# A four-layer graph network: a second edge sort with its scatter and gather replaced by one-hot products over a list of tile and span pairs

## Chip, cores, metric

The kernel runs on one core of one Trainium2 chip. The metric is the device time of one execution in microseconds (us); lower is better.

## What is computed

A graph has 12,500 nodes with 128 features each and 212,500 directed edges (`src`, `dst`), in the order of `dst`. Four layers follow each other; after each the result is added to x and layer-normalised over the features.

```python
def _L1_gnn_ref(...):                      # the layer whose sums are changed
    def _gin_layer(x, src, dst, W1, b1, g1, be1, W2, b2, g2, be2):
        agg = jax.ops.segment_sum(x[src], dst, num_segments=x.shape[0])
        h = (x + agg) @ W1 + b1            # 128 -> 32
        h = _bn(jnp.maximum(h, 0.0), g1, be1)
        h = _bn(h @ W2 + b2, g2, be2)      # 32 -> 128
        return jnp.where(h > 0, h, NEG_SLOPE * h)
    h = _gin_layer(x, src, dst, W1_0, ...)
    return _gin_layer(h, src, dst, W1_1, ...)
```

Layer 0 sums `edge_val * x[dst]` by `src` and puts two branches behind it. Layer 2 runs a small MLP on every edge (`x[src]`, `x[dst]`, `edge_attr`) and sums by `src`. Layer 3 is an attention over the edges of each `src`. So layers 0, 2 and 3 sum by `src` and look up `dst`; layer 1, which has two GIN layers inside, sums by `dst` and looks up `src`. Since W1 is linear, layer 1 is computed on z = x @ W1, which has 32 features; z is held as three bf16 parts that add up to it (96 columns, `z3`).

## The kernel before

**Tiles.** The nodes are 98 blocks of 128. The edges are sorted by the block of `src` into `edges_a`, in DRAM, as 1,760 tiles of 128 edges, each tile with edges of one block (its number is in `blk_a`); an edge's row holds 128 attributes, `src` within its block, `dst` and the weight (`pay_a` in SBUF). Groups of 4 tiles are the step of all passes: 440 steps.

**First sort** (up to L1505). DVE makes a one-hot of the block (1,661 columns, one instruction for each of the 98 blocks, L1454), PE counts it (L1055), a scan gives the starts. Then the places are computed in five parts of the columns (`PARTS`), for each part 98 times: DVE compares (L1512), PE makes three products (L1075 to L1077), DVE takes the result where the one-hot is set (L1502). POOL may start to scatter once the first part (160 columns) is placed. It issues one indirect DMA for 128 edges (L775), 1,661 of them, in groups of ten; SP reads the attributes for each group (L654 on) and ACT puts the rest of the row beside them (`stage`, L848).

**Layer 0** (`sum_step`). POOL gathers x rows by `dst` (L807), one indirect DMA per tile; PE multiplies with a one-hot of `src` (L1127), DVE adds the result to the block's sums (L1625). Between its steps DVE and PE do the **second sort** for layer 1, by the block of `dst` (`hist_b`, `place_b`, `take_b`).

**First GIN layer.** POOL splits z into its three parts (`split`, L787). In each of 440 steps SP broadcasts the tiles' `src` (L690), DVE turns it into a one-hot (L1868), PE looks up z of the block by a product (L1240, with a block number that it loads into registers), ACT writes the message (L912, L913), and POOL scatters it to its place in `rows_b`, one indirect DMA per tile (L822). Then SP reads `rows_b` back in 110 chunks (L708), DVE makes one-hots (L1887), and PE adds to the sums in PSUM (`chunk_sums`, L1261), three products of 32 columns per tile.

**Second GIN layer.** z goes to DRAM (`z_tab`), POOL gathers it in the second order, one indirect DMA per tile (L834), and PE adds it up (`gather_sum`, L1276). Between the two and after them stand the dense parts (`gin_pe`, `gin_act`, `gin_dve`: two batch norms and the products with W2 and the next W1).

**Layers 2 and 3** (`mlp`, `attend`) run over `edges_a` again with a gather per tile each (L807, q_tab and h_tab). Between the layers stand node phases of 14 steps.

The order of the work is that of the program on each engine; semaphores set by hand tie the engines together. POOL issues its 10,460 indirect DMAs one after the other.

## Time and profile before

| | us |
|---|---|
| median of 3 runs | 16622.23 |
| lowest and highest run | 16610.61, 16624.17 |
| span of the profiled execution, first to last instruction | 14549.9 |
| POOL busy in it | 10118.0 (70%) |
| DVE busy | 6490.2 (45%) |
| PE busy | 5642.2 (39%) |
| ACT busy | 2071.4 (14%) |

The profile has one execution. It gives its span; a device time of its own, beside the span, is not given, so the only figure for what lies around the span is the median less the span, 2072 us.
### The profile page before, as it was taken

To read this page: it belongs to the slowest core of one execution; us is meant where nothing else is said; L and a number is where in the kernel's file an instruction comes from. 1 tells how busy PE (TensorE), PEld (TensorE's weight loads), DVE (VectorE), ACT (ScalarE), POOL (GpSimd) and SP (SyncE) were. 2 spreads that over 40 slices of the span, in tenths; PEclk is the share of its full clock that TensorE was granted. 3 is DMA by queue.
4 is the path that set the end of the run, shared out by engine and by line. 5 is a ranking of instruction groups with operands and counts; after the bars stand their busy time and mean duration, and the time that the engine had idled before them with its cause. 6 is when DMAs were issued, how large, how long until landed. Compare 5 with 4: busy or idle time off the path is not lost.

```text
span 14549.9 us, 185642 instructions
## 1 busy us (share of the span) xinstructions
PE 5642.2 (39%) x42509; PEld 4641.8 (32%) x42510; DVE 6490.2 (45%) x25163; ACT 2071.4 (14%) x8809; POOL 10118.0 (70%) x10603
## 2 busy tenths in 40 slices
PE   7200002546655111111441111127888885444443
PEld 2000002333334100000441111127888884444442
DVE  9201113667765100000541111137888886656666
ACT  0000000000002111111010000015666662000000
POOL 4777777777774677777237777746777774777775
PEclk9655555768765555555555555559999996555555
DMA  4444449211112212211321111125555554333333
GB/s 109 127 126 140 127 141 81 53 50 52 52 51 61 54 46 46 46 46 44 92 52 20 20 20 20 20 51 132 131 131 131 131 130 113 80 80 79 80 80 86
DMA packets 1400883, 1138.59 MB, mean 78 GB/s; under 512 B 445673, under 2 KB 1261295, under 8 KB 1400143
## 3 DMA queue, kind: packets, MB, share of 16 engines
q1 hardware_dynamic: 1049493, 567.59, 16.8%
q0 software_dynamic: 335264, 554.74, 15.6%
q10 hardware_dynamic: 15778, 12.82, 0.3%
q14 instruction: 276, 2.26, 0.1%
q8 instruction: 72, 1.18, 0.0%
HBM read 871.76 MB, written 262.57 MB: 78 GB/s over the span
## 4 chain that ended last, share of the span: by engine, by line
POOL 58%; issue 19%; DVE 4%; PE 2%; DMA 1%; ACT 1%; DVEq 0%; SPq 0%; POOLq 0%; ACTq 0%
POOL work L807 34%; POOL rows_b L822 12%; POOL work L834 11%; DVE work L1887 2%; DMA x_tab<-work 0%; DVE work L1849 0%; DVE work L1855 0%; PE ps L1261 0%; DVE work L1801 0%; PE ps L1357 0%; PE ps L1224 0%; PE ps L1229 0%; DVE work L1941 0%; PE ps L1218 0%; DVE big L1632 0%
## 5 line engine op out<-in xcount | busy, mean ns | idle before, releaser
L807 POOL DMA_INDIRECT work<-q_tab,pay_a x1760 | 1673.5, 951 | 715.8 <-issue 535.1
L807 POOL DMA_INDIRECT work<-h_tab,pay_a x1760 | 1671.8, 950 | 673.5 <-issue 536.1
L807 POOL DMA_INDIRECT work<-in_x_dram,pay_a x1760 | 1709.4, 971 | 545.2 <-issue 536.0
L822 POOL DMA_INDIRECT rows_b<-work,big x1760 | 1706.7, 970 | 540.0 <-issue 536.2
L834 POOL DMA_INDIRECT work<-z_tab,work x1760 | 1662.8, 945 | 539.2 <-issue 536.0
L775 POOL DMA_INDIRECT edges_a<-work x1660 | 1607.4, 968 | 567.0 <-issue 508.7
L1625 DVE TENSOR_TENSOR big<-big,ps 128x128 f32 (+1 forms) x5280 | 1494.7, 283 | 940.8 <-PE ps L1127 531.9
L1868 DVE TENSOR_SCALAR work<-work,iota_p 128x512 bf16<-128x512 bf16 (+1 forms) x1320 | 560.3, 425 | 2220.0 <-PE ps L1240 1946.5
L1431 PE MATMUL ps<-work 128*128 128x129 f32 x3520 | 916.9, 441 | 1220.5 <-DVE work L1617 1220.5
L1127 PE MATMUL ps<-work 128*128 128x128 f32 x3520 | 749.3, 379 | 1376.2 <-DMA work<-in_x_dram,pay_a 995.5
L1431 PEld LDWEIGHTS ps<-work 128*128 128x128 f32 x3520 | 788.2, 329 | 1256.5 <-DVE big L1625 1162.3
L1958 DVE TENSOR_SCALAR work<-iota_h,lo_chunk 128x128 bf16<-128x128 bf16 x1760 | 329.3, 270 | 1862.9 <-PE ps L1276 1858.1
L1617 DVE TENSOR_SCALAR work<-iota,work 128x128 f32<-128x128 f32 x3520 | 1134.8, 364 | 16.2
L1127 PEld LDWEIGHTS ps<-work 128*128 128x128 f32 x3520 | 639.3, 272 | 1561.9 <-issue 1495.5
L1276 PE MATMUL ps<-work 128*128 128x32 bf16 x5280 | 284.3, 194 | 1916.2 <-DMA work<-z_tab,work 1879.9
L1240 PE MATMUL ps<-big,work 128*128 x1760 | 292.0, 259 | 1878.7 <-ACT work L913 1864.6
L1276 PEld LDWEIGHTS ps<-work 128*128 128x128 bf16 x5280 | 238.2, 108 | 1962.4 <-issue 1957.7
L1393 PE MATMUL ps<-wc,work 128*128 128x128 f32 x3520 | 715.5, 285 | 355.8 <-ACT work L1010 187.1
L1240 PEld LDWEIGHTS ps<-big,work 128*128 128x128 bf16 x1760 | 183.3, 104 | 1987.4 <-issue 1946.7
L1394 PE MATMUL ps<-work,ident 128*128 128x128 f32 x3520 | 681.8, 275 | 0.0
L1395 PE MATMUL ps<-big,work 128*128 x3520 | 681.8, 275 | 0.0
L1393 PEld LDWEIGHTS ps<-wc,work 128*128 128x128 f32 x3520 | 533.1, 191 | 448.9 <-issue 223.6
(346 smaller groups left out, 12240.8 us busy)
## 6 DMA issues: line engine op xcount, KB each, us to landing
work<-lo_rows SPq DMA_DIRECT2D x1320, 128.0 KB
work<-edges_a SPq DMA_DIRECT2D x440, 256.0 KB
work<-in_edge_attr_dram SPq DMA_DIRECT2D x166, 640.0 KB, 5.1
rows_b<-work SPq DMA_DIRECT2D x80, 550.0 KB, 7.5
work<-rows_b SPq DMA_DIRECT2D x110, 400.0 KB, 3.2
work<-in_x_dram,pay_a POOLq DMA_INDIRECT x1760
rows_b<-work,big POOLq DMA_INDIRECT x1760
work<-z_tab,work POOLq DMA_INDIRECT x1760
```

Source lines behind the costliest of these rows:

```text
L775: pool.indirect_dma_start(out=edges_a, out_offset=bass.IndirectOffsetOnAxis(ap=stage_pos[:, k, j:j + 1], axis=0), in_=stage_a[:, k, j, :], ...
L807: pool.indirect_dma_start(out=ring[:, at:at + width], out_offset=None, in_=table, in_offset=bass.IndirectOffsetOnAxis(ap=pay[:, e, 1:2], a ...
L822: pool.indirect_dma_start(out=rows_b, out_offset=bass.IndirectOffsetOnAxis(ap=pos_b[:, s * G + j:s * G + j + 1], axis=0), in_=message[:, k ...
L834: pool.indirect_dma_start(out=rows_h[:, at:at + H3], out_offset=None, in_=z_tab, in_offset=bass.IndirectOffsetOnAxis(ap=pay_b_i[:, e, 1:2] ...
L1127: m = pe.matmul(ps[:, kk % 4, j * D:(j + 1) * D], lhsT=onehot[:, kk % 4, j], rhs=rows[:, at:at + D], start=True, stop=True)
L1393: pe.matmul(o, lhsT=attr_t[:, kk % 2, j * P:(j + 1) * P], rhs=wc[:, 2, :], start=True, stop=False)
L1394: pe.matmul(o, lhsT=ident[:, :], rhs=rows[:, at:at + D], start=False, stop=False)
L1395: m = pe.matmul(o, lhsT=onehot_t[:, kk % 2, j * P:(j + 1) * P], rhs=p_all[:, bass.ds(bl[j] * D, D)], start=False, stop=True)
L1431: m = pe.matmul(ps[:, sums + j // 2, (j % 2) * 256:(j % 2) * 256 + D + 1], lhsT=onehot[:, kk % 4, j], rhs=rows[:, at:at + D + 1], start=Tr ...
L1617: ins = dve.tensor_scalar(onehot[:, k % 4, j], iota[:, :], pst[:, k, j, 0:1], scale, ALU.is_equal, ALU.mult)
L1625: dve.tensor_tensor(o, o, tile_sums, ALU.add).then_inc(p.acc, 1)
L1868: dve.tensor_scalar(turned, lo_bc[:, k % 4], iota_p[:, 0:1], None, ALU.is_equal).then_inc(p.oht, 1)
```

## The change

**One sort.** The first sort now ranks by a cell, the block of `src` and the span of `dst` (25 spans of 512 nodes). Counting: DVE makes one-hots of 98 blocks and of 25 spans for 50 columns at a time (34 batches), PE multiplies them column by column (1,661 products of 98 x 25, L1183). Placing goes along with the scatter, a group of ten columns at a time (`ask`, `place`, `look`; L1598, L1616, L1196): SP broadcasts the keys of the group to all partitions (655 KB), DVE counts the edges of the same cell before each edge (ten instructions of 128 to 640 columns that also sum, L1623), PE fetches the start of each edge's cell (ten products) and DVE picks it (ten instructions of 50 columns that also sum, L1628). POOL waits for `ranks.placed` before each group's ten scatters. ACT issues the attribute loads now, and between the groups DVE, PE and ACT do the part of layer 0 that was done beside the scatter before (`own_step`, 14 of them, every eighth group from group 40).

**A list of pairs.** A tile's edges are in the order of their spans. Every pair of a tile and a span that has edges in it gets an entry; each span's entries are filled up to a multiple of 16. The bound on the list is 4,512 entries: 1,128 steps of 4, in 282 groups of 16. The list is made during layer 0 (`cell_list` to `pair_list`; 50 comparisons of 2,304 columns, L1841, with 18 small products each) in place of `hist_b` and `place_b`. After layer 0 POOL gathers the tile rows for it (36 indirect DMAs), and ACT and PE turn them.

**The two GIN sums.** For each step of 4 pairs (`pair_sums`) SP broadcasts the pairs' `src` (128 KB), DVE makes the turned one-hot (L2013) and four one-hots of 128 x 512 of `dst` in its span (L2016), PE looks up z (four products of 96 columns, L1381), ACT copies the messages (L1041), and PE multiplies them with the one-hots into 96 x 512 sums (four products of 512 columns, L1390). Every four steps DVE adds these to the sums (L2026). The sums of a node's own z come first (`own_columns`), and the dense part begins with `fold3`, 28 products of 448 columns in f32, in the place of 25 transposes. `rows_b`, `z_tab`, their scatters, gathers and reads are gone. All 4,512 entries are worked through in each layer.

```diff
+QG = 16
+QUADS_G = QG // 4
+PAIR_GROUPS = -(-((E + NB * (P - 1)) // P + NB * (SPANS - 1) + SPANS * (QG - 1)) // QG)
+PAIR_GROUPS += PAIR_GROUPS % 2
+PAIRS = PAIR_GROUPS * QG
+QUADS = PAIRS // 4
+QB = -(-PAIRS // P)
+QB += QB % 2
+HALF_B = QB // 2
...
+sp.wait_ge(ranks.stored, 32)
+for q in range(SGROUPS + 1):
+    wait(sp, ranks.placed, q - 3)
+    n = min(SG, COLS - q * SG)
+    sp.dma_start(row_bc[:, q % 4, 0:n, :].rearrange("p j f -> p (j f)"),
+                 key_rows[q * SG:q * SG + n, :].rearrange("j f -> (j f)").partition_broadcast(P)).then_inc(ranks.row_in[q % 4], 16)
...
+def pair_in(l):
+    def step(s, k, u):
+        wait(sp, sums.oht, s + (l * QUADS - 3))
+        sp.dma_start(pair_bc[:, k % 4, :], pair_lo[bass.ds(s * (4 * P), 4 * P)].partition_broadcast(P)).then_inc(sums.lo[k % 4], 16)
+    run_steps(sp, QUADS, RING, 0, step)
...
-for s in range(GROUPS):
-    k = s % RING
-    pool.wait_ge(z1.staged, 2 * s + 2)
-    for j in range(G):
-        pool.indirect_dma_start(out=rows_b, out_offset=bass.IndirectOffsetOnAxis(ap=pos_b[:, s * G + j:s * G + j + 1], axis=0),
-                                in_=message[:, k, j, :], in_offset=None).then_inc(got[k], 16)
...
-for c in range(TILES // CHUNK):
-    if c >= 5:
-        pool.wait_ge(p2.mm, 2 * GROUPS + (c - 4) * (CHUNK // G))
-    for j in range(CHUNK):
-        at, e = (c % 5 * CHUNK + j) * H3, c * CHUNK + j
-        pool.indirect_dma_start(out=rows_h[:, at:at + H3], out_offset=None, in_=z_tab,
-                                in_offset=bass.IndirectOffsetOnAxis(ap=pay_b_i[:, e, 1:2], axis=0)).then_inc(got[c % 5], 16)
+for s in range(SGROUPS):
+    k = s % 2
+    pool.wait_ge(order.attr[k], s // 2 * 16 + 16)
+    pool.wait_ge(order.staged, s * 3 + 3)
+    pool.wait_ge(ranks.placed, s + 1)
+    for j in range(SG):
+        pool.indirect_dma_start(out=edges_a, out_offset=bass.IndirectOffsetOnAxis(ap=pos_a[:, s % POS, j:j + 1], axis=0),
+                                in_=stage_a[:, k, j, :], in_offset=None).then_inc(order.scat[k], 16)
...
+pool.wait_ge(pairs.list, 1)
+pool.wait_ge(pairs.stored, 64)
+for b in range(QB):
+    pool.indirect_dma_start(out=got_rows(b), out_offset=None, in_=tile_rows,
+                            in_offset=bass.IndirectOffsetOnAxis(ap=tile_sel[:, b:b + 1], axis=0)).then_inc(pairs.got, 16)
...
+def message_out(l):
+    def step(s, k, u):
+        act.wait_ge(sums.smm, s + (l * QUADS + 1))
+        wait(act, sums.mm, s + (GROUPS + l * QUADS - 3))
+        act.activation(pair_msg[:, k % 4, :], ps[:, k % 4, 0:4 * H3], ACT.Copy).then_inc(sums.staged, 1)
+    run_steps(act, QUADS, RING, 0, step)
...
-def chunk_sums(s, k, u):
-    bl = load_blocks(ONLY_PE, blk_b, s, 2 * CHUNK)
-    for h in range(2):
-        c = 2 * s + h
-        pe.wait_ge(s1.oh, c * 4 + (GROUPS + 4))
-        pe.sem_inc(begun, 1)
-        for n in range(CHUNK // G):
-            for j in range(G):
-                for f in range(3):
-                    m = pe.matmul(ps_flat[:, bass.ds(bl[h * CHUNK + n * G + j] * H, H)], lhsT=onehot_h[:, 4 * h + n, j],
-                                  rhs=chunk[:, (2 * k + h) % 5, n * G + j, f * H:(f + 1) * H], start=False, stop=True, skip_group_check=True)
-            m.then_inc(s1.mm, 1)
...
+for c in range(width):
+    at = (m_ % 2 * PER + c // CG) * SPANS
+    m = pe.matmul(ps[0:NB, m_ // 2 % 8, at:at + SPANS], lhsT=hot[m_ % 3][:, 0:NB, c], rhs=hot[m_ % 3][:, NB:KEYS, c],
+                  start=c % CG == 0, stop=c % CG == CG - 1 or c == width - 1)
...
+def look(q):
+    pe.wait_ge(o.asked, q + 1)
+    wait(pe, o.placed, q - 3)
+    for j in range(min(SG, COLS - q * SG)):
+        m = pe.matmul(look_bank(q)[:, j * LOOK:(j + 1) * LOOK], lhsT=asked[0:NB, q % 2, j * P:(j + 1) * P],
+                      rhs=split_a[0:NB, q % 2 * 2 + j // CG, :], start=True, stop=True)
+    m.then_inc(o.look, 1)
...
+def pair_sums(l):
+    def step(s, k, u):
+        if live(s, QUADS):
+            bl = load_blocks(ONLY_PE, blk_row, s)
+            pe.wait_ge(sums.oht, s + (l * QUADS + 1))
+            wait(pe, sums.staged, s + (l * QUADS - 3))
+            for j in range(4):
+                m = pe.matmul(ps[:, k % 4, j * H3:(j + 1) * H3], lhsT=pair_turn[:, k % 4, j * P:(j + 1) * P], rhs=z3_flat[:, bass.ds(bl[j] * H3, H3)], start=True, stop=True)
+            m.then_inc(sums.smm, 1)
+        g, (kk, gu) = s - 2, back(k, u, 2, RING)
+        if live(g, QUADS):
+            pe.wait_ge(sums.staged, g + (l * QUADS + 1))
+            pe.wait_ge(sums.oh, g + (GROUPS + l * QUADS + 1))
+            if kk % QUADS_G == 0:
+                wait(pe, sums.acc, gu * 2 + (kk // QUADS_G + TILES + l * PAIR_GROUPS - 1))
+            for j in range(4):
+                m = pe.matmul(ps[0:H3, 4 + kk // QUADS_G, :], lhsT=pair_msg[:, kk % 4, j * H3:(j + 1) * H3], rhs=pair_hot[:, kk % 4, j, :],
+                              start=kk % QUADS_G == 0 and j == 0, stop=kk % QUADS_G == QUADS_G - 1 and j == 3)
+            m.then_inc(sums.mm, 1)
+    run_steps(pe, QUADS, RING, 2, step)
...
+for c in range(PCH):
+    for h in range(4):
+        at = h * PART + c * PW
+        m = pe.matmul(ps[:, c, 0:PW], lhsT=fold3[0:H3, h, :], rhs=acc_t[0:H3, at:at + PW], start=h == 0, stop=h == 3)
...
-if q < PLACED:
-    a, b = PARTS[q // NB]
-    s = q % NB
-    wait(dve, o.took, q - 7)
-    dve.tensor_scalar(eq_p[:, q % 8, 0:b - a], hi_h[:, a:b], iota[:, s:s + 1], None, ALU.is_equal).then_inc(o.eqp, 1)
-if q >= DEEP:
-    take_place(q - DEEP)
...
+for m in range(HBATCHES):
+    at, w = m * HB, min(HB, COLS - m * HB)
+    wait(dve, o.hist, m - 2)
+    dve.tensor_tensor(hot[m % 3][:, 0:NB, 0:w], hi_h[:, at:at + w].unsqueeze(1).to_broadcast([P, NB, w]), key_tab[:, 0:NB, 0:w], ALU.is_equal)
+    dve.tensor_tensor(hot[m % 3][:, NB:KEYS, 0:w], span_h[:, at:at + w].unsqueeze(1).to_broadcast([P, SPANS, w]), key_tab[:, NB:KEYS, 0:w],
+                      ALU.is_equal).then_inc(o.hot, 1)
...
+n = min(SG, COLS - q * SG)
+for g in range(-(-n // CG)):
+    k, first = q % 2 * 2 + g, first_a[0:NB, :, q * (SG // CG) + g]
+    ch.post(dve.tensor_scalar(quarter[0:NB, g, :], first, small[0:NB, 4:5], 0.25, ALU.add, ALU.mult))
+dve.tensor_scalar(asked[:, q % 2, 0:n * P].rearrange("p (j e) -> p j e", e=P), row_bc[:, q % 4, 0:n, P:2 * P], iota_p[:, 0:1], None, ALU.is_equal)
+ch.sync()
+for g in range(-(-n // CG)):
+    ch.post(dve.tensor_copy(split_a[0:NB, q % 2 * 2 + g, 0:SPANS], quarter[0:NB, g, :]))
+ch.sync()
+for g in range(-(-n // CG)):
+    at = split_a[0:NB, q % 2 * 2 + g, :]
+    ins = dve.tensor_tensor(at[:, SPANS:LOOK], quarter[0:NB, g, :], at[:, 0:SPANS], ALU.subtract)
+ins.then_inc(o.asked, 1)
+def place(q):
+    n = min(SG, COLS - q * SG)
+    dve.wait_ge(o.look, q + 1)
+    for j in range(n):
+        c, jj = q * SG + j, j % CG
+        w = (jj + 1) * P
+        dve.scalar_tensor_tensor(out=unread(q, j).rearrange("p (j e) -> p j e", e=P), in0=row_bc[:, q % 4, j - jj:j + 1, 0:P], scalar=cell_f[:, c:c + 1],
+                                 in1=earlier[:, (CG - 1 - jj) * P:CG * P].rearrange("p (j e) -> p j e", e=P),
+                                 op0=ALU.is_equal, op1=ALU.mult, accum_out=later[:, q % 2, j:j + 1])
+    for j in range(n):
+        c = q * SG + j
+        ins = dve.scalar_tensor_tensor(out=junk_x[:, P + j * LOOK:P + (j + 1) * LOOK], in0=iota_k[:, :], scalar=span_f[:, c:c + 1], in1=look_bank(q)[:, j * LOOK:(j + 1) * LOOK],
+                                       op0=ALU.is_equal, op1=ALU.mult, accum_out=found[:, q % 2, j:j + 1])
+    ch(ins)
+    if q >= POS:
+        dve.wait_ge(order.scat[q % 2], ((q - POS) // 2 + 1) * (16 * SG))
+    dve.scalar_tensor_tensor(out=pos_a[:, q % POS, 0:n], in0=found[:, q % 2, 0:n], scalar=4.0, in1=later[:, q % 2, 0:n], op0=ALU.mult, op1=ALU.add).then_inc(o.placed, 1)
...
+def compare(i):
+    h, k = divmod(i, SPANS)
+    wait(dve, pairs.mm, i - 3)
+    dve.tensor_scalar(cmp_q[i % 4][0:NB + 1, :], pair_h[0:NB + 1, :], pair0_h[0:NB + 1, h, k:k + 1], None, ALU.is_ge).then_inc(pairs.cmp, 1)
...
+def pair_sums(l):
+    def step(s, k, u):
+        if live(s, QUADS):
+            if k % 4 == 0:
+                dve.tensor_copy(pair_at[:, k * 4:k * 4 + 16], pair_dst[:, bass.ds(s * 4, 16)]).then_inc(sums.pst, 1)
+                dve.wait_ge(sums.pst, u * 2 + (GROUPS + l * (QUADS // 4) + k // 4 + 1))
+            dve.wait_ge(sums.lo[k % 4], u * 32 + (KEY_ROWS[k % 4] + l * per_sum + k // 4 * 16 + 16))
+            wait(dve, sums.smm, s + (l * QUADS - 3))
+            dve.tensor_scalar(pair_turn[:, k % 4, :], pair_bc[:, k % 4, :], iota_p[:, 0:1], None, ALU.is_equal).then_inc(sums.oht, 1)
+            wait(dve, sums.mm, s + (GROUPS + l * QUADS - 3))
+            for j in range(4):
+                ins = dve.tensor_scalar(pair_hot[:, k % 4, j, :], iota_s[:, :], pair_at[:, k * 4 + j:k * 4 + j + 1], None, ALU.is_equal)
+            ins.then_inc(sums.oh, 1)
+        g, (kk, gu) = s - 7, back(k, u, 7, RING)
+        if kk % QUADS_G == 0 and live(g, QUADS):
+            half = kk // QUADS_G
+            group = gu * 2 + half
+            v = load_span(group)
+            dve.wait_ge(sums.mm, g + (GROUPS + l * QUADS + QUADS_G))
+            wait(dve, sums.acc, group + (TILES + l * PAIR_GROUPS))
+            at = acc_t[0:H3, bass.ds(v * SPAN, SPAN)]
+            dve.tensor_tensor(at, at, ps[0:H3, 4 + half, :], ALU.add).then_inc(sums.acc, 1)
+    run_steps(dve, QUADS, RING, 7, step)
```

**Order on DVE.** In the pair loop of the changed kernel the last of each four steps, with the addition, is (work is the region with the one-hots, ps the PSUM, pair_dst the turned rows of `dst`):

```order
L2013 TENSOR_SCALAR work<-work,iota_p 128x512 [waits z_smm,lo_in3]
L2016 TENSOR_SCALAR work<-work 128x512 [waits sum_mm]
L2016 TENSOR_SCALAR work<-work 128x512 x3
L2000 TENSOR_LOAD work
L2026 ISA [waits sum_acc,sum_mm]
L2026 TENSOR_TENSOR big<-big,ps 96x512
```

The other three steps have the first three rows alone. Before, the chunk sums' part of DVE was, for two steps of four tiles:

```order
L1883 SCALAR_TENSOR_TENSOR work<-work 128x16 [waits z_payload]
L1887 TENSOR_SCALAR work<-iota_h,lo_chunk 128x128 [waits sum_mm]
L1887 TENSOR_SCALAR work<-iota_h,lo_chunk 128x128 x3
L1887 TENSOR_SCALAR work<-iota_h,lo_chunk 128x128 [waits sum_mm]
L1887 TENSOR_SCALAR work<-iota_h,lo_chunk 128x128 x3
```

A step has five instructions of 512 columns where it had four of 128, and no DMA of POOL stands beside it.

**Order on PE.** One step of the pair loop; ISA rows set the address of the next product from a register:

```order
L636 TENSOR_LOAD work
L1381 ISA [waits z_oht]
L1381 MATMUL ps<-big,work 128x96
L1381 ISA
L1381 MATMUL ps<-big,work 128x96
L1381 ISA
L1381 MATMUL ps<-big,work 128x96
L1381 ISA
L1381 MATMUL ps<-big,work 128x96
L1390 MATMUL ps<-work 96x512 [waits sum_oh,z_staged]
L1390 MATMUL ps<-work 96x512 x3
```

Before, the message pass had the first nine of these rows (L1240) for each step; the four products of 512 columns are new in the loop.

**Order on DVE while POOL scatters.** Before, the placing was a pair of rows for each of 98 blocks and five parts:

```order
L1512 TENSOR_SCALAR big<-big,iota 128x510 [waits sort_took]
L1502 COPY_PREDICATED big<-big,ps 128x510 [waits sort_took,sort_pos]
```

Now a group of ten columns has, in this order (a second five rows of L1623, like the first, are left out):

```order
L1605 TENSOR_SCALAR big<-work,small 98x25 [waits rank_asked,lo_in0]
L1605 TENSOR_SCALAR big<-work,small 98x25
L1606 TENSOR_SCALAR big<-pay_a,iota_p 128x1280
L1609 CAST big<-big 98x25 [waits s_sort]
L1609 CAST big<-big 98x25
L1613 TENSOR_TENSOR big<-big 98x25 [waits s_sort]
L1613 TENSOR_TENSOR big<-big 98x25
L1623 SCALAR_TENSOR_TENSOR big<-pay_a,big 128x128 [waits rank_look]
L1623 SCALAR_TENSOR_TENSOR big<-pay_a,big 128x256
L1623 SCALAR_TENSOR_TENSOR big<-pay_a,big 128x384
L1623 SCALAR_TENSOR_TENSOR big<-pay_a,big 128x512
L1623 SCALAR_TENSOR_TENSOR work,big<-pay_a,big 128x640
```

and, behind the second five, `L1628 SCALAR_TENSOR_TENSOR big<-big,ps 128x50 x10` and one row of L1633 that lets POOL go on. The placing has moved from ahead of the scatter to beside it.

## Rows read from the trace of the kernel before

**Rows 1.** The page's head, and the first line of its chain of waits.
```profile
span 14549.9 us, 185642 instructions
...
POOL 58%; issue 19%; DVE 4%; PE 2%; DMA 1%; ACT 1%; DVEq 0%; SPq 0%; POOLq 0%; ACTq 0%
```
**Rows 2.** Costliest groups on POOL: busy us, mean ns, idle before with its releasers.
```profile
L807 POOL DMA_INDIRECT work<-in_x_dram,pay_a x1760 | 1709.4, 971 | 545.2 <-issue 536.0 <-DMA pay_a<-edges_a 9.2
L822 POOL DMA_INDIRECT rows_b<-work,big x1760 | 1706.7, 970 | 540.0 <-issue 536.2 <-ACT work L912 3.8
L834 POOL DMA_INDIRECT work<-z_tab,work x1760 | 1662.8, 945 | 539.2 <-issue 536.0 <-DMA z_tab<-big 3.2
```
**Rows 3.** Stretches: length, busy us (count) of PE, PEld, DVE, ACT, POOL; clock, DMA share, GB/s.
```profile
0.00:184.30 184.30, 117.08 (x722) 58.90 (x723) 170.54 (x364) 2.20 (x9) 27.34 (x31) 0.90 0.50 99
184.30:2320.80 2136.50, 324.72 (x1486) 144.81 (x1485) 438.31 (x1202) 87.37 (x676) 1608.36 (x1662) 0.57 0.45 130
2320.80:4570.00 2249.20, 1188.06 (x5118) 810.76 (x5118) 1468.67 (x4512) 0.00 (x0) 1709.32 (x1760) 0.69 0.30 53
4570.00:4770.00 200.00, 124.67 (x624) 110.44 (x624) 140.61 (x568) 84.93 (x185) 27.41 (x56) 0.64 0.24 69
4770.00:7014.00 2244.00, 298.16 (x1766) 185.85 (x1766) 164.12 (x436) 263.31 (x878) 1706.73 (x1760) 0.50 0.19 46
7014.00:7405.00 391.00, 241.11 (x5268) 227.93 (x5269) 301.55 (x1870) 39.09 (x220) 0.00 (x0) 0.50 0.41 116
7405.00:7493.00 88.00, 68.09 (x299) 58.66 (x298) 50.02 (x100) 37.17 (x57) 30.74 (x56) 0.56 0.14 28
7493.00:9697.00 2204.00, 287.55 (x5289) 239.67 (x5287) 329.33 (x1836) 0.23 (x1) 1662.77 (x1760) 0.50 0.12 20
9697.00:9872.00 175.00, 99.55 (x537) 78.29 (x537) 126.37 (x394) 71.60 (x101) 0.30 (x1) 0.79 0.43 121
```
**Rows 4.** DVE groups by form: busy us, mean ns of one.
```profile
L1658 DVE TENSOR_SCALAR big<-big,iota 128x1760 bf16<-128x1760 bf16 x98 | 70.4, 718 | 0.1
L2006 DVE TENSOR_TENSOR work<-ps,gamma 128x512 f32<-128x512 f32 x440 | 290.1, 659 | 0.1
L1463 DVE TENSOR_TENSOR big<-big 128x1660 f32<-128x1660 f32 x1 | 1.9, 1890 | 0.0
```
**Rows 5.** Timeline of DVE, three stretches: start us, length us of the x instructions.
```profile
302.00 0.33 DVE L1512 TENSOR_SCALAR big<-big,iota 128x510 bf16<-128x510 bf16 x1
302.26 0.71 DVE L1502 COPY_PREDICATED big<-big,ps 128x510 f32<-128x510 uint16 x1
...
1225.07 1.89 DVE L1592 TENSOR_SCALAR big<-big 128x128 f32<-128x128 f32 x7
...
7018.41 2.69 DVE L1887 TENSOR_SCALAR work<-iota_h,lo_chunk 128x128 bf16<-128x128 bf16 x16
```
**Rows 6.** Timeline of one step of the message pass.
```profile
5608.37 0.49 ACT L912 ACTIVATE work<-ps 128x384 bf16<-128x384 f32 x1 [4.91 <-DMA rows_b<-work,big]
...
5609.27 0.66 PE L1240 MATMUL ps<-big,work 128*128 x4 [4.85 <-ACT work L913]
5609.97 0.35 DVE L1868 TENSOR_SCALAR work<-work,iota_p 128x512 bf16<-128x512 bf16 x1 [5.15 <-PE ps L1240]
...
5610.49 0.33 SPq L690 DMA_DIRECT2D work<-lo_rows  x1
```
**Rows 7.** PE: the placing stretch with its granted clock; 512-column groups by form.
```profile
184.00:460.00 276.00, 249.09 (x1143) 0.99 0.42 120
...
L1055 PE MATMUL ps<-big,onecol 128*128 128x512 bf16 x294 | 72.5, 390 | 26.4 <-DVE big L1454 26.4
L1249 PE MATMUL ps<-big,ident 128*128 128x512 f32 x24 | 15.7, 821 | 40.4 <-ACT work L913 39.9 <-ACT big L996 0.5
```
**Rows 8.** Timeline of ACT: an activation that also sums, and the next one.
```profile
10607.10 0.27 ACT L1019 ACTIVATE square<-ps 128x128 f32<-128x128 f32 x1
10607.26 0.20 ACT L1019 ACTIVATION_READ_ACCUMULATOR square<-ps 128x1 f32 x1
10607.35 0.28 ACT L1019 ACTIVATE square<-ps 128x128 f32<-128x128 f32 x1
```
**Rows 9.** Matmuls of 32 columns in the chunk sums.
```profile
7021.39 2.17 PE L1261 MATMUL ps<-work 128*128 128x32 bf16 x48 [39.59 <-DVE work L1887]
```

1290 lines of the change are left out of this document (643 added, 647 removed).

## The prediction

> **What bounds the kernel.** The page's head and its chain of waits come first: POOL is 58% of the chain and "issue" 19%, everything else is 7% or less [rows 1]. The costliest groups say what POOL does: indirect DMAs, each busy for 0.945 to 0.971 us, with 536 us of idle time per 1,760 of them put down to "issue", 0.30 us each [rows 2]. So POOL starts one every 1.25 to 1.27 us, and nothing on another engine ends those gaps. The windows by stage [rows 3] show where the span goes: 184.3 us ahead of the scatter, 2136.5 scatter, 2249.2 layer 0, 200 node phase, 2244 messages with their scatter, 391 chunk sums, 88 dense, 2204 gathers of z, 175 dense and node phase; then layers 2 and 3, which the change leaves as they are. In the scatter DVE is busy for 438 of 2136 us and PE for 325: both have room.
>
> The span is 14549.9 us, the median 16622.23. No device time of the profiled execution is given, so I make the sum as differences of its span and carry the 2072 us around it over unchanged.
>
> **Prices.** DVE, bf16, one source and scalars: 16 instructions of 128 columns in 2.69 us are 0.168 each; of 510 columns the next instruction starts 0.26 after it [rows 5]; 1,760 columns take 0.718 [rows 4]. So 512 columns cost 0.27. The slope is (0.26-0.168)/382 = 0.24 ns a column by the first two, (0.718-0.26)/1250 = 0.37 by the last two; I use 0.28. f32: 7 of 128 columns in 1.89 us, 0.27 each [rows 5]; 1,660 columns with two f32 sources take 1.89 [rows 4]; the adding of PSUM to SBUF, 512 columns, 0.66 [rows 4]. From 0.27 for 128 columns I split off about 0.14 fixed and 1.04 ns a column, which the 1,660 columns bear out, (1.89-0.14)/1660 = 1.05. PE: four products with register addresses take 0.66 us, 0.165 each [rows 6], in a stretch with its clock at 0.50 [rows 3]; 512 columns bf16 take 72.5/294 = 0.247 busy, in the stretch where the clock is high [rows 7]: at 2.4 GHz about 0.22 from one to the next, so at 1.2 GHz about 0.43. ACT writes a message in 0.49, SP issues a broadcast in 0.33 [rows 6].
>
> **Part 1: the two GIN sums.** The 4,512 pairs are all worked through, so a step's price decides. By engine, for four pairs:
> - DVE: 5 x 0.27 = 1.35; per four steps an address copy with its wait, estimated 0.25, and the addition 0.66, so 0.23 a step: 1.58.
> - PE's array: four look-ups of 96 columns, about 0.2 in all at full clock, and 4 x 0.22: 1.07. With the register loads and address settings (0.165 x 4, about 0.6 for the loads) the sequencer needs about 1.5.
> - ACT 0.6 (0.49 and a wait), SP 0.5; POOL nothing.
>
> DVE is the longest, and PE's sequencer stands just under it. Nothing is hidden under POOL any more, since POOL does nothing here. For two engines so near each other that hand four buffers back and forth I add 0.12: **1.70 us a step**, 1128 x 1.70 = 1918 us a layer. The bounds: 1.55, if the fixed part of an instruction is smaller than the four-buffer rows say; and 2.0, if queueing costs 0.4. Against it: first layer, -2244 - 391 + 1918 = **-717**. Second, -2204 + 1918 = **-286**. So two thirds of POOL's work in these stages is gone, and the gain is only a third of it.
>
> **Part 2: placing beside the scatter.** A group of ten columns must not take longer than POOL's ten scatters, 10 x 1.263 = 12.6 us [rows 2]. DVE's group: L1623 ten times, 3,840 f32 columns: 10 x 0.14 + 3840 x 1.04 ns = 5.4. L1628 ten times 50 columns: 1.9. Both also write their sums; the nearest rows are ACT's: an activation starts at 10607.10, its accumulator read at 10607.26 and the next activation at 10607.35 [rows 8]: of the read's 0.20 only 0.09 is added. Twenty of them, 1.8. `ask`: one of 1,280 bf16 columns 0.5 and six small at 0.17, 1.5. The last instruction and waits 0.4. Sum 11.0, under 12.6. One group in eight also carries an `own_step` of about 15 us of DVE's work: eight groups need 8 x 11.0 + 15 = 103 us against POOL's 101. They are level; what falls behind is caught up at 1.6 us a group before the next and after the last. I take **+20** for the stage, between 0 and +328 (rival 3). The broadcasts of 655 KB a group come on top of DMA engines that are busy for 0.45 of the stage [rows 3], and have three groups' time ahead.
>
> The Trainium skill, "VectorE: DVE Perf Modes", section "Two Vector instructions with no wait between them", states that an instruction that also writes out its accumulator runs as two, the main one and the read. It speaks against this change, and no DVE row here shows it. Without it the group would be 9.2 us by the sum above and the +20 would be 0; the +20 goes by ACT's pair of rows, as said.
>
> **Part 3: counting.** What stands ahead of the scatter today, 98 one-hots with 1,661 columns of counting and the first part's placing, is 184.3 us [rows 3]. Now 34 batches of 123 x 50 = 6,150 columns on DVE. Two bf16 sources: no such row, so from both sides: at the one-source slope of 0.28 ns a column 60 us, at the f32 two-source rate of 1.14 ns [rows 4] 236. PE's 1,661 products of 25 columns: 48 of 32 columns in 2.17 us are 45 ns each [rows 9], 75 us, up to 0.165 each [rows 6], 274. DVE and PE overlap; I take 150, near the middle, since two sources in bf16 lie between the two rows. With the keys, the scan of 2,450 columns x 34/10 (8,325 in all, 9) and the first group's look-up, 11, the first scatter starts at about 220: **+36**.
>
> The skill's same page, section "The perf-mode tier table", gives a two-source bf16 instruction twice the f32 rate, which would make the counting 34 x 3.5 = 119 us and the sum 31 lower.
>
> **Part 4: the list of pairs, in layer 0.** A step of four gathers is POOL's 5.05 us; DVE is busy for 1469 of 2249 us there and PE for 1188 [rows 3], and the work of the second sort leaves as that of the list comes. 50 comparisons of 2,304 columns, about 0.8 each, and 900 products of four columns fit: **0**. If DVE were full, +50. After layer 0 come 36 gathers (46 us of POOL, partly beside the 200 us of the node phase), their turning and the tables, +12 for what waits and +22 for `own_columns`, the copying of 98 blocks to 96 rows: **+34**. The bounds are 10 and 80.
>
> **Part 5: the dense parts.** `fold3`: 28 products of 448 f32 columns. Twelve f32 products of 512 columns show 15.7 us busy for 24 records, so 28 of 448 are 16 to 32 us [rows 7]; less the 25 transposes, +16. With the second layer's `own_columns` +13 and no z_tab to write (-5): first **+24**. The second, where a wait for z_tab doesn't exist: **+16**.
>
> **Sum.** 36 + 20 + 0 + 34 - 717 + 24 - 286 + 16 = -873. The span becomes 13,677, the time 16622 - 873 = 15,749.
>
> **The rivals.**
> 1. *Slower: PE's clock stays at 1.2 GHz in the pair loops.* For: in the chunk sums PE is busy for 241 of 391 us and its clock is 0.50 [rows 3]; in the pair loop it waits at each step for DVE or ACT. Then a step is 4 x 0.165 + 4 x 0.43 = 2.38 on PE, it becomes the bound at 2.4, and 2256 x 0.7 = 1579 us are lost: 17,330. It decides from 1.70 + 873/2256 = 2.09 us a step. Also layer 0 has 0.69. Against: the placing stretch, where products of up to 512 columns follow each other with waits for DVE between them as here, has 0.99 [rows 7]; the chunk sums' products have 32 columns.
> 2. *The queues cost more:* register loads, semaphores and the four buffers make it 2.0 a step. PE's own sum is near DVE's, and a late broadcast holds both. 2256 x 0.3 = 677: 16,430.
> 3. *DVE becomes the bound in the scatter.* If an accumulator read isn't overlapped (ACT's read alone 0.20, not 0.09 [rows 8]), a group is 11.0 + 20 x 0.11 = 13.2; 167 x 13.2 + 260 for the rest (14 own steps and the stage's ends) = 2464 against 2136 + 20: +308, 16,060. For: the sums of the two are only 1.6 us a group apart. Against: POOL's own distance of 1.25 us is steady, and an f32 row of 0.27 already holds its write.
> 4. *The time around the span falls with the indirect DMAs.* They go from 10,460 to 6,985, by a third; if the 2072 us were theirs, 690 go with them: 15,060. For: nothing in the trace says what it is. Against: nothing ties it to them either, and the distance of the DMAs inside the span stays as it is.
>
> The change can also fail to do what it says: if the pair loop still waited for POOL; but no POOL instruction stands in it, so I give that no chance of its own.
>
> **How the numbers follow.** Forecast 0.53 (15,750, its own range 15,400 to 16,050, with 1.55 and 1.83 a step), slower by the clock 0.08, queues 0.12, DVE in the scatter 0.15, time outside the span 0.10, and 0.02 left. A measurement of this kernel can tell about 0.2%, 33 us, from no change; of the cases only the first rival and the tail of the second are beyond that on the slow side: slower 0.09, same 0.01, faster 0.90. The range goes to the queues' 16,430 above; below, to 15,150, since 1.55 a step gives 15,410 and the fourth rival would need a bit more.
>
> **What would show it.** In the profile of the changed kernel: L2016 9,024 times, each 0.27 after the last; the two pair loops 1,918 us each, with DVE at over 85% there and PE's clock near 1.0 (0.5 is the first rival); L1390's products 0.22 apart. The first scatter at 220 us. In the scatter POOL waiting for `ranks.placed` by less than 1% of the stage; an average group above 12.6 us on DVE is the third rival. The gathers of layer 2 starting at 9872 - 873 = 9,000. And the median less the span again 2,072. The prediction is wrong if a step of the pair loop is over 2.09 us, or if a stage that I took as covered, the list of pairs or the broadcasts of keys, ends POOL's waits.

## The result and the profile after

| | before | changed | ratio (95% interval) |
|---|---|---|---|
| median, us | 16622.46 | 15473.67 | 0.931 (0.9299 to 0.9321) |
| span of the profiled execution | 14549.9 [rows 1] | 15486.0 | |
| its own time | not given | 15487.77 | |

The change is 1149 us faster; 873 were forecast. The two spans can't be compared: that of the changed kernel is its time less 1.8 us, that of before was 2072 us under its median. The kernel before, unchanged, takes 14,550 to 14,660 us in two groups of runs (here called the quick condition) and 16,610 to 16,650 in three (the slow one), so every ratio below is taken beside runs of the kernel before in the same group. The profile of the rows ahead of the prediction is of the quick condition, the times shown with it are of the slow one, and so is the result above. The ratio is 0.931 in both (0.9315, interval 0.9300 to 0.9331, in the quick one).

So the terms of the prediction, which came from the quick condition, are held against a profile of the changed kernel in that condition (its span is 13576.7, that of before 14557.0). Its stretches; the columns are those of [rows 3]: count and first place, scatter, layer 0, node phase and list, first pair loop, dense part with the second `own_columns`, second pair loop, dense and node phase:

```profile
0.00:384.10 384.10, 313.83 (x1733) 311.71 (x1734) 177.44 (x236) 49.41 (x31) 24.68 (x28) 0.54 0.25 60
384.10:2608.90 2224.80, 173.42 (x1960) 142.69 (x1960) 1584.88 (x8261) 72.36 (x511) 1697.87 (x1661) 0.51 0.51 152
2618.90:4849.30 2230.40, 929.93 (x4452) 814.66 (x4453) 1087.10 (x4064) 4.12 (x8) 1694.21 (x1759) 0.51 0.32 54
4849.30:5067.00 217.70, 146.29 (x761) 130.64 (x760) 150.99 (x602) 105.86 (x240) 64.51 (x93) 0.62 0.30 85
5067.00:6828.00 1761.00, 1648.52 (x9019) 894.35 (x9020) 1697.26 (x6202) 554.01 (x1128) 0.00 (x0) 1.00 0.32 84
6828.00:6938.00 110.00, 88.11 (x415) 69.91 (x413) 44.36 (x73) 42.85 (x68) 30.69 (x56) 0.67 0.02 5
6938.00:8701.00 1763.00, 1671.94 (x9030) 894.73 (x9028) 1698.46 (x6206) 554.72 (x1130) 0.00 (x0) 1.00 0.32 84
8701.00:8892.50 191.50, 116.78 (x572) 84.78 (x572) 124.57 (x391) 71.08 (x100) 0.00 (x0) 0.83 0.39 111
```

In a pair loop DVE is busy for 1697 of 1761 us and PE's clock is 1.00. Between the same marks (first and last indirect DMA of a stage, first one-hot of a pair loop) in the quick profiles of both kernels:

| stage | before | changed | difference | forecast |
|---|---|---|---|---|
| up to the first scatter | 183.1 | 384.1 | +201 | +36 |
| scatter | 2127.1 | 2224.8 | +98 | +20 |
| layer 0 | 2248.5 | 2230.4 | -18 | 0 |
| to the first GIN sum | 206.6 | 217.6 | +11 | +34 |
| first GIN sum, dense | 2722.7 | 1872.3 | -850 | -693 |
| second GIN sum, dense, node | 2384.3 | 1953.3 | -431 | -270 |
| layers 2 and 3, rest | 4674.6 | 4684.2 | +10 | 0 |
| sum | | | -980 | -873 |

Costliest groups that answer to [rows 2] and [rows 4], by form, of the changed kernel in the quick condition (busy us, mean ns, idle before):

```profile
L2016 DVE TENSOR_SCALAR work<-work 128x512 bf16<-128x512 f16 x9024 | 2557.6, 346 | 1.2 <-PE ps L1390 1.2
L859 POOL DMA_INDIRECT edges_a<-work,big x1660 | 1697.9, 1023 | 550.6 <-issue 505.3 <-DMA edges_a<-big,fill_pos 24.0 <-DMA work<-in_edge_attr_dram 17.6
L1183 PE MATMUL ps<-work 128*98 128x25 bf16 x1661 | 304.7, 342 | 1.8 <-ACT big L936 1.8
L1569 DVE TENSOR_TENSOR work<-work 128x4900 bf16<-128x4900 bf16 x33 | 89.5, 2713 | 172.1 <-PE ps L1183 172.1
L1570 DVE TENSOR_TENSOR work<-work 128x1250 bf16<-128x1250 bf16 x33 | 26.5, 803 | 0.0
```

**Counting.** PE is busy for 304.7 us and idle for 1.8; a product starts every 304.7/1661 = 0.183 us. The middle of the counting, same columns as above, with a clock of 0.50:

```profile
30.00:330.00 300.00, 300.00 (x1638) 300.00 (x1638) 105.27 (x64) 38.01 (x16) 0.00 (x0) 0.50 0.15 28
```
DVE, which makes the one-hots, waits 172.1 us for PE. What is long in a product is the load of its weights, in ns (least, median, most), of L1183 and, for comparison, of L1201, whose weights have 128 columns:

```profile
L1183 PEld LDWEIGHTS ps<-work x1661: 260/280/284, 28.0 to 332.3; 128*98 128x98 bf16 x185
L1201 PEld LDWEIGHTS ps<-big x1661: 95/119/151, 359.4 to 3309.0; 98*128 98x128 bf16 x185
```

After the last product (332 us) come the scan, the fill and the wait of 24.0 us for the fill to land, and the first scatter is at 384.1.

**The pair loop**, timeline of the quick profile: the rows of DVE follow each other without a gap but for the last one, where it waits 0.21 for its own copy of the positions, once in four steps.

```profile
5606.77 0.35 DVE L2013 TENSOR_SCALAR work<-work,iota_p 128x512 bf16<-128x512 bf16 x1
5606.93 0.49 ACT L1041 ACTIVATE work<-ps 128x384 bf16<-128x384 f32 x1 [0.97 <-PE ps L1381]
5607.03 1.14 DVE L2016 TENSOR_SCALAR work<-work 128x512 bf16<-128x512 f16 x4
...
5608.08 0.35 DVE L2013 TENSOR_SCALAR work<-work,iota_p 128x512 bf16<-128x512 bf16 x1
5608.20 0.60 PEld L1390 LDWEIGHTS ps<-work 128*96 128x96 bf16 x4
5608.21 1.06 PE L1390 MATMUL ps<-work 128*96 128x512 bf16 x4
...
5609.99 0.17 DVE L2009 CAST work<-pair_dst 128x16 f32 x1
5610.37 0.35 DVE L2013 TENSOR_SCALAR work<-work,iota_p 128x512 bf16<-128x512 bf16 x1 [0.21 <-DVE work L2009]
```

A step without the addition is 5608.08 - 5606.77 = 1.31 us, five instructions of 0.26; the mean is 1.562 (a loop of 1762 us by 1,128 steps).

**The first measurement** (slow condition) has one thing that the quick one doesn't. What POOL and ACT waited for in its scatter stage (us in total, times, longest):

```profile
POOL edges_a L859 <- DMA work<-in_edge_attr_dram: 677.6, 15, 51.7
POOL edges_a L859 <- issue: 497.5, 1619, 3.8
POOL edges_a L859 <- DVE big L1633: 89.5, 22, 10.7
...
ACT big L970 <- DVE big L1666: 942.7, 14, 70.2
```

and one of the 13 waits of 47 to 52 us, first ACT's timeline, then POOL's:

```profile
1207.30 0.20 ACT L952 ACTIVATE work<-big 128x10 f32<-128x10 f32 x1
1276.56 0.21 ACT L970 ACTIVATE big<-big 128x7 f32<-128x7 f32 x1 [69.05 <-DVE big L1666]
1276.56 0.37 ACTq L958 DMA_DIRECT2D work<-in_edge_attr_dram  x1
...
1230.34 0.95 POOL L859 DMA_INDIRECT edges_a<-work,big  x1 [0.30 <-issue]
1281.40 1.94 POOL L859 DMA_INDIRECT edges_a<-work,big  x1 [50.11 <-DMA work<-in_edge_attr_dram]
```

ACT now issues the attribute loads. Four groups ahead of each `own_step` it waits for DVE's variance (L969), and the next group's load stands behind that wait. When DVE isn't four groups ahead of POOL, the wait outlasts the groups that are loaded, and POOL stops at 1231 us until the load has landed. That this is the cause was tested by moving the wait (the runs with the later square root, below).

### The profile page after: what moved, and what is told of

It reads as the page before. It is cut to its first block and busy times, and to the rows that moved or that the text cites. A ratio compares the mean times of both kernels' runs of the same rounds, so it can differ in the third digit from the quotient of the medians.

```text
span 15486.0 us, 239207 instructions
## 1 busy us (share of the span) xinstructions
PE 8370.8 (54%) x49340; PEld 6322.0 (41%) x49341; DVE 9889.6 (64%) x39917; ACT 2938.7 (19%) x9899; POOL 6932.9 (45%) x7116
## 5 line engine op out<-in xcount | busy, mean ns | idle before, releaser
L2016 DVE TENSOR_SCALAR work<-work 128x512 bf16<-128x512 f16 x9024 | 2564.3, 349 | 1.5 <-PE ps L1390 1.5
L1390 PE MATMUL ps<-work 128*96 128x512 bf16 x9024 | 2392.2, 388 | 4.0 <-DVE work L2016 0.2
L859 POOL DMA_INDIRECT edges_a<-work,big x1660 | 1687.3, 1016 | 1291.4 <-DMA work<-in_edge_attr_dram 677.6
L1265 PE MATMUL ps<-work 128*128 128x128 f32 x3520 | 908.5, 435 | 1536.5 <-DVE work L1757 671.4
L1041 ACT ACTIVATE work<-ps 128x384 bf16<-128x384 f32 x2256 | 1105.5, 490 | 2414.4 <-PE ps L1381 2414.4
L1201 PE MATMUL ps<-big 98*128 98x50 f16 x1661 | 99.1, 218 | 2550.9 <-DVE big L1613 1520.4
L1972 DVE TENSOR_SCALAR work<-work,iota_p 128x512 f32<-128x512 bf16 (+1 forms) x880 | 383.5, 436 | 1703.8 <-remote 1629.3
L1265 PEld LDWEIGHTS ps<-work 128*128 128x128 f32 x3520 | 777.4, 322 | 1657.6 <-issue 1428.0
L1381 PE MATMUL ps<-big,work 128*128 x9024 | 1335.4, 212 | 199.5 <-DVE work L2013 182.5
L1381 PEld LDWEIGHTS ps<-big,work 128*128 128x128 bf16 x9024 | 862.5, 96 | 1175.2 <-issue 890.9
L1540 PEld LDWEIGHTS ps<-work 128*128 128x128 f32 x3520 | 788.1, 329 | 1115.2 <-DVE big L1765 651.3
L1390 PEld LDWEIGHTS ps<-work 128*96 128x96 bf16 x9024 | 927.7, 122 | 559.4 <-issue 14.2
L1201 PEld LDWEIGHTS ps<-big 98*128 98x128 bf16 x1661 | 78.5, 118 | 2573.0 <-DVE big L1613 1537.2
```

The costliest lines, as they stand in the source:

```text
L859: pool.indirect_dma_start(out=edges_a, out_offset=bass.IndirectOffsetOnAxis(ap=pos_a[:, s % POS, j:j + 1], axis=0), in_=stage_a[:, k, j, : ...
L1041: act.activation(pair_msg[:, k % 4, :], ps[:, k % 4, 0:4 * H3], ACT.Copy).then_inc(sums.staged, 1)
L1265: m = pe.matmul(ps[:, kk % 4, j * D:(j + 1) * D], lhsT=onehot[:, kk % 4, j], rhs=rows[:, at:at + D], start=True, stop=True)
L1381: m = pe.matmul(ps[:, k % 4, j * H3:(j + 1) * H3], lhsT=pair_turn[:, k % 4, j * P:(j + 1) * P], rhs=z3_flat[:, bass.ds(bl[j] * H3, H3)], s ...
L1390: m = pe.matmul(ps[0:H3, 4 + kk // QUADS_G, :], lhsT=pair_msg[:, kk % 4, j * H3:(j + 1) * H3], rhs=pair_hot[:, kk % 4, j, :], start=kk % Q ...
L1540: m = pe.matmul(ps[:, sums + j // 2, (j % 2) * 256:(j % 2) * 256 + D + 1], lhsT=onehot[:, kk % 4, j], rhs=rows[:, at:at + D + 1], start=Tr ...
```

## Experiments

**Two conditions.** The kernel before, unchanged, twice:

> The kernel before, unchanged, to see where the 2072 us lie that its median has above the span of the profile. Theory A (the time lies inside the stages: the profiled execution shown was free of stalls that the timed runs have): the span here is about 16,620, within 10 us of its own time, and the indirect DMAs of the unchanged layers 2 and 3 take longer than 2214 and 2206 us, like the 2680 and 2555 of the changed kernel. Theory B (the time lies around the span): a span near 14,550 again, with its time 2072 above it.

Measured: 14559.04 us, span 14557.0. Neither theory as written: the span is near 14,550, but so is the time. Nothing lies around the span.

> The kernel before, once more, for a profile under the conditions in which it takes 16,620 to 16,640 us. If it takes that here: Theory A says that its span is within 10 us of its time and that the 2072 us lie as stalls inside the stages in which POOL issues indirect DMAs, more per stage in layers 2 and 3 (about 450 and 350, as in the changed kernel) than in those with little on PE and DVE. Rival B: they lie in all stages alike, by the number of indirect DMAs (0.198 us each, 350 us a pass). If it takes 14,560 here, nothing new is expected.

Measured: 16642.05 us, span 16640.0. Theory A holds. Stretches of layer 2 and layer 3 in this profile, to be held against 2207.5 and 2206.4 us in the quick one:

```profile
11108.10:13792.90 2684.80, 2113.69 (x15562) 1952.37 (x15563) 1667.42 (x6889) 1334.18 (x6040) 1758.15 (x1759) 0.94 0.41 107
13953.50:16507.10 2553.60, 1034.01 (x5232) 917.58 (x5231) 1348.69 (x6088) 89.51 (x436) 1670.33 (x1760) 0.50 0.31 69
```

| stage length, us | before quick | before slow | changed quick | changed slow |
|---|---|---|---|---|
| scatter | 2127.1 | 2447.7 | 2224.8 | 2954.7 |
| layer 0 | 2248.5 | 2551.3 | 2230.4 | 2509.4 |
| messages / pair loop 1 | 2241.6 | 2505.4 | 1762.6 | 1761.4 |
| z gathers / pair loop 2 | 2198.1 | 2507.0 | 1761.7 | 1762.0 |
| layer 2 | 2207.5 | 2684.8 | 2210.8 | 2678.1 |
| layer 3 | 2206.4 | 2553.6 | 2212.0 | 2554.5 |

In the kernel before, the slow condition costs each of the six stages in which POOL issues indirect DMAs 264 to 477 us, 2021 of the 2083 us between the two profiles; the other 62 lie in the node phases between and behind them, and the stretch ahead of the scatter (183.1 and 183.0 us) and that from the last message to the first z gather (481.1 in both) have none of it. A pair loop has none either; the scatter of the changed kernel has 730. The change takes 264 + 309 = 573 us of it away and gives 730 - 321 = 409 back in the scatter; that is why the ratios are alike. What the condition is stays open. In its traces consecutive instructions of an engine often start 1.40 us apart, or 0.70 or 2.10: from 700 to 2300 us in the changed kernel DVE has 220 distances of 1.30 to 1.45 us and 49 of 2.0 to 2.2, and in the quick profile none of either; in the message stage of the kernel before, from 5500 us on, PE has 217 of 1.30 to 1.45 in 2000 us, and none in the quick profile. It wasn't tried whether this is a matter of the supply of instructions. The two quick groups ran on two chips and two of the slow ones on two others, so whether the condition belongs to the chip is open too.

**The changed kernel again**, quick:

> The changed kernel, unchanged, beside the kernel before on the same chip. Theory A (the 1104 us of stalls in the first measurement of the before/after pair, 2072 in the kernel before, belong to the conditions of that measurement and not to the kernels): if the kernel before takes 14,560 here, this one takes 13,565 (the run with two one-hots plus what its pair loops saved, 13,359 + 116 + 90), a ratio of 0.931 again; if the kernel before takes 16,620 here, 15,470. Rival B (the changed kernel always stalls once per own_step): 14,100 or more beside 14,560.

Measured: 13577.78 beside 14576.12, ratio 0.9315. Theory A; B is out, there is no wait for an attribute load over 10.4 us in it. And slow:

> The changed kernel, unchanged, as the mark for the run with the earlier address copy on the same chip: 13,565 to 13,580 us beside 14,560 of the kernel before, or 15,470 beside 16,620.

Measured: 15493.77 beside 16635.61, ratio 0.931 (0.9295 to 0.9326).

**ACT's wait four groups later.**

```diff
-                i, at = divmod(s + 4 - OWN_AT, OWN_GAP)
+                i, at = divmod(s - OWN_AT, OWN_GAP)
                 if at == 0 and 0 <= i < NSTEPS:
                     act.wait_ge(own.var, i + 1)
...
```

> Changed kernel, ACT's wait for DVE's own_step stands four groups later in ACT's order, behind the attribute load of the same group. Theory A (the 12 stalls of POOL of about 49 us, once in eight groups, come from attribute loads queued on ACT behind its wait for own_step): they go, the scatter stage falls from 2953 us to about 2350, the time to about 14,900. Rival B (DVE's own slow stretches hold the placing and the wait on ACT only shows them): the stage stays within 150 us of 2953, and POOL's waits move from the attribute load to ranks.placed. DVE, not ACT, would then be the bound.

Measured: 13575.12, but beside 14563.87: the quick condition, in which POOL isn't stalled, so it tells nothing of the theory. Its times were expected for the slow one.

> ACT's wait for own_step four groups later, now timed beside the unchanged changed kernel. Theory A: where POOL is not stalled by the attribute loads (12 to 15 waits of 49 us absent in the changed kernel's trace) this is within 0.2% of it; where they are there, 500 us or more faster. Rival B: slower by 14 x a few us everywhere, since DVE waits longer for the square root.

Measured: 13581.94 beside 13577.78 of the unchanged one: equal within 0.2%. The other half of Theory A needs the slow condition, below.

**Two one-hots of four**, and its counterpart, **two sum products of four**:

```diff
-                            m = pe.matmul(..., rhs=pair_hot[:, kk % 4, j, :], ...)
+                            m = pe.matmul(..., rhs=pair_hot[:, kk % 4, j // 2 * 2, :], ...)
...
-                        for j in range(4):
+                        for j in range(0, 4, 2):
                             ins = dve.tensor_scalar(pair_hot[:, k % 4, j, :], ...)
```

> Changed kernel; in the pair loops DVE makes two of the four one-hots of a step and PE uses each twice, so the sums of the two GIN layers are not those of the reference. Theory A (DVE bounds the loop at 1.56 us a step): a step falls to PE's price, between 1.07 (array) and 1.50 (its dispatch as predicted), so each loop by 70 to 550 us. Rival B (the hand-over of buffers or PE's dispatch bounds it): the loops stay within 2% of 1762 us.

Measured: 13359.48; a step is 1.459 us in the first loop and 1.481 in the second. Theory A, near its lower end. DVE's work was cut by 0.52 us and only 0.08 to 0.10 came: PE, busy for 98% of the stretch from 5500 to 6500 us, now bounds the loop at 1.46 to 1.48, near the 1.5 of the prediction, and DVE bounds the changed kernel's loop by the little in between.

```diff
-                        for j in range(4):
+                        for j in range(0, 4, 3):
                             m = pe.matmul(ps[0:H3, 4 + kk // QUADS_G, :], ...)
```

> Changed kernel; in the pair loops PE makes two of the four 512-column products of a step, so the sums of the two GIN layers leave out half of the pairs. Theory A (DVE bounds): the loops stay at 1762 us within 1%. Rival B (PE's array or its dispatch bounds): the loops fall by up to 2 x 0.22 x 1128 = 500 us each. What its clock does with fewer columns is seen too: if it falls to 0.5 and the loops still take 1762, the first rival of the prediction is too high for this kernel.

Measured: 15510.49 beside 16635.61; loops of 1761 and 1760 us. Theory A. A stretch of 1000 us inside the first loop:

```profile
6300.00:7300.00 1000.00, 838.07 (x3848) 381.21 (x3847) 964.65 (x3527) 314.77 (x641) 0.00 (x0) 0.78 0.32 84
```

The clock falls to 0.78 and the loop keeps its time; PE, with half of the long products, is busy for 838 of 1000 us and still keeps up. This isn't the first rival's case, which has all of the products.

**POOL makes the fourth one-hot.** DVE makes three; PE waits for both.

```diff
...
+                    wait(pool, sums.mm, s + (GROUPS + l * QUADS - 3))
+                    pool.tensor_scalar(pair_hot[:, k % 4, 3, :], iota_s[:, :], pair_at[:, k * 4 + 3:k * 4 + 4], None, ALU.is_equal).then_inc(own.relu, 1)
...
+                        pe.wait_ge(own.relu, g + (NSTEPS + l * QUADS + 1))
...
-                        for j in range(4):
+                        for j in range(3):
                             ins = dve.tensor_scalar(pair_hot[:, k % 4, j, :], ...)
```

> Changed kernel; POOL, idle in the pair loops, makes the fourth one-hot of each step. Theory A (DVE bounds a step at 1.56, PE at 1.46 as the run with two one-hots showed): a step takes 1.46 to 1.48, the two loops lose 190 us. Rival B (POOL's own instruction and its use of what it shares with DVE cost more): POOL needs over 1.5 us for 512 columns or DVE's instructions beside it lengthen, and the loops are slower than 1762 us.

Measured: 14694.17 beside 13577.78 of the changed kernel, 1116 slower; a step is 2.064. Rival B, in both of its halves. The group on POOL (busy us, mean ns, idle before):

```profile
L915 POOL TENSOR_SCALAR work<-work 128x512 bf16<-128x512 f16 x2256 | 3637.6, 1626 | 1035.0 <-DVE work L2021 903.1 <-PE ps L1402 115.5 <-issue 15.0
```

and in the timeline DVE's three one-hots beside it, which take 1.45 on average here and 0.87 in the changed kernel:

```profile
7002.92 1.65 DVE L2028 TENSOR_SCALAR work<-work 128x512 bf16<-128x512 f16 x3
```

What POOL would need with DVE at rest wasn't measured.

**DVE instructions beside POOL's DMAs.** In the changed kernel's scatter POOL's DMA takes 1.023 us on average, before 0.968 (L775). Sorted by what DVE does meanwhile, counted over the trace (profile of the kernel with the later square root, quick): the 783 that overlap an L1623, with two SBUF sources, take 1.095 on average; the other 877 take 0.961, those beside L1628 alone, whose second source is PSUM, 0.958. Tested in the kernel before:

```diff
                 turned_onehot(z1, k, u, onehot_th[:, k])
+                for q in range(4):
+                    ins = dve.scalar_tensor_tensor(out=spare[:, q, :], in0=onecol[:, :], scalar=1.0, in1=onecol[:, :], op0=ALU.is_equal, op1=ALU.mult)
...
                 ins.then_inc(p2.oh, 1)
+                for q in range(4):
+                    ins = dve.tensor_scalar(spare[:, q, :], onecol[:, :], 1.0, None, ALU.is_equal)
```

> Kernel before, with four added DVE instructions of 256 columns in each of 440 steps: two SBUF sources (the form of L1623) beside the message scatter, one SBUF source (bf16, the form of L2016) beside the gathers of z. Theory A (POOL's indirect DMA is lengthened while DVE runs an instruction with two SBUF sources, as 1.095 us beside L1623 and 0.957 without say): the message scatter's DMAs lengthen from 0.970 by about 0.05 on average, the stage by 40 to 120 us, the gathers of z stay at 0.945. Rival B (the key broadcasts on the DMA queues lengthen them): both stages unchanged.

Measured: 14651.56 beside 14576.12, in one run. Its groups, for [rows 2]'s L822 and L834:

```profile
L823 POOL DMA_INDIRECT rows_b<-work,big x1760 | 1774.5, 1008 | 540.2 <-issue 536.3 <-ACT work L914 3.8
...
L835 POOL DMA_INDIRECT work<-z_tab,work x1760 | 1682.1, 956 | 539.3 <-issue 536.2 <-DMA z_tab<-big 3.2
```

The message stage went from 2241.6 to 2309.8 us (+68), within Theory A's 40 to 120. The z stage wasn't unchanged: +19, 0.956 for 0.945, so one source lengthens POOL's DMA as well, by less per added us of DVE (19 us for 228 more of DVE's busy time, 68 for 580: 0.08 and 0.12). So the first half of Theory A holds, and its second half, with two sources alone, does not. Rival B is out as the only cause, since no key broadcast runs here; what share broadcasts have in the changed kernel's scatter wasn't tested.

**The address copy one step earlier.**

```diff
+                dve.tensor_copy(pair_at[:, 0:16], pair_dst[:, 0:16]).then_inc(sums.pst, 1)
...
                         if k % 4 == 0:
-                            dve.tensor_copy(pair_at[:, k * 4:k * 4 + 16], pair_dst[:, bass.ds(s * 4, 16)]).then_inc(sums.pst, 1)
...
+                        if k % 4 == 3:
+                            half = (k // 4 + 1) % 2
+                            dve.tensor_copy(pair_at[:, half * 16:half * 16 + 16], pair_dst[:, bass.ds((s + 1) * 4, 16)]).then_inc(sums.pst, 1)
```

> Changed kernel; in the pair loops DVE copies the 16 span positions of the next four steps one step earlier, so that it doesn't wait 0.21 us for its own copy. Theory A (DVE bounds the step, PE stands at 1.46 to 1.48): 282 x 0.21 = 60 us less in each loop, 120 in all, a step of 1.51. Rival B (PE's dispatch and the hand-over already limit the mean step): less than 40 us in all.

Measured: 15326.78 beside 15493.77 of the changed kernel and 16635.61 of before, ratio 0.9212 (0.9196 to 0.9227). Theory A, with a step of 1.484 and a loop 88 us shorter, not 60. The wait of 0.21 was not all that the copy's place cost: from the copy's start to the next one-hot's it was 5610.37 - 5609.99 = 0.38 us, and here the next instruction starts 0.08 after the copy (6499.85 and 6499.93 us in its timeline), which makes 282 x 0.30 = 85 us a loop. In its profile DVE is busy for 1000.00 of 1000.00 us:

```profile
6300.00:7300.00 1000.00, 980.14 (x5400) 534.99 (x5399) 1000.00 (x3713) 330.63 (x676) 0.00 (x0) 1.00 0.34 88
```

**Both edits together.**

> Changed kernel with both edits, the address copy one step earlier and ACT's wait for own_step four groups later. Under the conditions with 14,560 for the kernel before: 13,577 - 176 = 13,400, the second edit worth nothing. Under those with 16,630 Theory A (the waits of 49 us for attribute loads come from ACT's order): 15,327 less 400 to 600 = 14,830, as they go with the edit. Rival B (DVE's own slow stretches hold the scatter): within 150 us of 15,327, POOL's waits now for ranks.placed.

Measured: 14927.76 beside 16637.66, ratio 0.8972 (0.8957 to 0.8987): the lowest ratio here; its time in the quick condition wasn't measured. It fell in the slow condition, so it is the test that the later square root lacked. With the early copy alone the scatter takes 2970.6 us, with both 2554.3; the time differs by 399, at the edge of the 400 to 600 expected. POOL's waits in the stage with the early copy alone:

```profile
POOL edges_a L859 <- DMA work<-in_edge_attr_dram: 680.4, 15, 51.3
POOL edges_a L859 <- issue: 496.0, 1615, 3.0
POOL edges_a L859 <- DVE big L1633: 105.8, 22, 10.7
```

and with both edits:

```profile
POOL edges_a L859 <- issue: 489.4, 1579, 3.9
POOL edges_a L859 <- DVE big L1633: 363.6, 76, 17.5
POOL edges_a L859 <- DMA edges_a<-big,fill_pos: 24.8, 1, 24.8
POOL edges_a L859 <- DMA work<-in_edge_attr_dram: 10.7, 2, 7.1
```

The attribute waits are gone, 670 us; 258 of them come back as waits for the placing. Theory A for the cause, and a share of Rival B for what stood behind it.

## Why the prediction was right, and where it was not

- **What bounds the kernel**: right. POOL was the bound; in the two stages that lost its work, DVE is.
- **Part 1**: right in mechanism, mis-sized. The step is 1.562, not 1.70, near the lower bound of 1.55. The 0.12 for handing over buffers wasn't there (DVE is busy for 96% of the loop), and five instructions take 1.31, not 1.35. 1128 x 0.138 = 156 us a loop is the whole gap in both GIN rows of the table (-850 for -693, -431 for -270). PE's price of about 1.5 was right (1.46 to 1.48 when it bounds; how much of that is its address settings no run shows), and so were its clock (1.00) and the dense terms of part 5: the first dense stretch is 110 us against 88 [rows 3], +22 for +24, the second 191.5 against 175.
- **Part 2**: the sum of a DVE group was too high and the stage's cost still too low. A group from L1633 to L1633 takes 8.7 us (1250.39 to 1259.12 in the first measurement's timeline; the median in the quick profile is 8.8), not 11.0, and DVE is busy for 1585 of the stage's 2225 us. The ranking instructions, quick profile:

```profile
1508.44 0.62 DVE L1623 SCALAR_TENSOR_TENSOR big<-pay_a,big 128x384 bf16<-128x384 f16 x1
1508.98 0.08 DVE L1623 DVE_READ_ACCUMULATOR big<-pay_a,big 128x1 f32 x1
1508.98 0.75 DVE L1623 SCALAR_TENSOR_TENSOR big<-pay_a,big 128x512 bf16<-128x512 f16 x1
1509.66 0.08 DVE L1623 DVE_READ_ACCUMULATOR big<-pay_a,big 128x1 f32 x1
1509.66 0.88 DVE L1623 SCALAR_TENSOR_TENSOR work<-pay_a,big 128x640 bf16<-128x640 f16 x1
```

  From one to the next with 384 columns 0.54 and with 512 0.68: that is 0.14 + 1.04 ns a column, with nothing left over for the read. That is the price which the prediction took from f32 rows, though these sources have 16 bits. By the Trainium skill's "VectorE: DVE Perf Modes", section "Two Vector instructions with no wait between them", such an instruction is two, the main one and the read, and the trace agrees: there is a row of 0.08 us for each read. But the read's time lies beside the next one's, so the 1.8 us taken from ACT's pair [rows 8] were not there, and the 9.2 of the sum without them was the nearer value. The third rival, a DVE-bound scatter, didn't come in the quick condition (POOL waited 3.7 us for the placing). What the sum left out is that POOL's DMA gets longer, 1660 x (1.023 - 0.968) = 91 of the 98 us, and the DMAs beside DVE's two-source instructions are the long ones.
- **Part 3**: wrong, +201 for +36, the largest miss. The step that failed is "DVE and PE overlap; I take 150, near the middle". DVE needs 34 x (2.71 + 0.80) = 119 us: 2.71 us for 4,900 columns are 0.55 ns a column, half of the 1.14 [rows 4]. The Trainium skill's "VectorE: DVE Perf Modes", section "The perf-mode tier table", gives a two-source bf16 instruction twice the f32 rate, and the trace agrees. But PE needs 305, over the 274 that the prediction had as its upper bound from [rows 6]; of two engines in a pipeline the longer one counts, and the middle of a range belongs to neither. Why a product of 25 columns costs 0.183 us, where one of 96 columns costs 0.165 or less [rows 6] and one of 32 costs 0.045 [rows 9], was not tested. The clock is 0.50 in all three, and each product of [rows 9] has a weight load of its own too (0.105 us by the median). The weight loads differ: 0.280 us in L1183, with 98 columns that lie 50 elements apart in `hot`, and 0.196 to 0.203 in the pair loop's L1390, with 96 columns side by side, in the first loads, at a clock of 0.50 (5071 to 5075 us), where those of L1381, with 128 columns, take 0.144 to 0.151. So weights of fewer than 128 columns, or their distance, or both can be the cause. The scan took 17.5, not 9, and the 24 us for the fill were not in the sum.
- **Part 4**: +11 and -18 for +34 and 0. The list is covered by layer 0; the 18 us are POOL's DMA at 0.963 for 0.973, 1760 times.
- **The 2072 us**: "carry the 2072 us around it over unchanged" was wrong in substance. They lie inside the stages, and were of another condition than the profile. The fourth rival, that they fall with the indirect DMAs, was right on where they go in the two GIN stages (573 us) and missed what the scatter gives back (409). That leaves 164 us, and with small differences elsewhere 169 of the 1149, where it had 690.
- **The missed wait**: the prediction never followed the attribute loads, which move to ACT's queue, behind ACT's wait for `own_step`. It costs nothing measurable in the quick condition and about 400 us in the slow one, where taking it out made the stage 416 us shorter.

Costs were set too low by 165 (part 3), 78 (part 2) and 10 (the rest), gains by 318 in the GIN stages and 41 in layer 0 and the list. That is 107, and with the 169 of the condition 276: the 15,750 against 15,474. It lies inside its range by luck, because large terms missed on opposite sides; term by term the gains and the costs were off by 359 and 253.

## What to carry to other kernels

Of two engines in a pipeline, price both and take the longer one; a number in the middle of a range belongs to neither. When a DMA issue moves to another engine's queue, list the waits that stand ahead of it there, since a load behind a wait for a later stage ties the producer to the consumer. And hold a profile's span against its own time before a difference to a median is carried over.

## What the runs showed of the hardware

- Products of 25 columns, each with its own weights, keep PE busy for 304.7 us almost without a break (1.8 us idle), with its clock at 0.50 (1.2 GHz); one starts every 0.183 us.
- At a clock of 0.50 PE loads bf16 weights of 128 columns in 0.104 to 0.151 us, of 96 columns in 0.196 to 0.203, and of 98 columns that lie 50 elements apart in 0.280.
- From one DVE instruction to the next, a TENSOR_TENSOR with two bf16 sources takes about 0.55 ns a column, a SCALAR_TENSOR_TENSOR with two 16-bit sources 1.04, and the read of its sum adds nothing.
- POOL needs 1.63 us for a one-hot of 512 columns, beside DVE, which makes one in 0.26 without POOL; POOL stretches three of DVE's from 0.87 to 1.45 us on average.
- In the changed kernel's scatter POOL's indirect DMA takes 1.095 us beside L1623, with two SBUF sources, and 0.961 otherwise. Four added DVE instructions a step lengthen it from 0.970 to 1.008 with two such sources and from 0.945 to 0.956 with one.
- A pair loop with half of the sum products has PE's clock at 0.78 instead of 1.00 and the same length.
- One and the same kernel took 14,559 and 16,642 us; 2021 of the 2083 us lie in the stages with POOL's indirect DMAs, the rest in the node phases. The pair loops of the changed kernel have none of it.
